# Layer 2 experts: a third buffer of gathered rows, and gathers and index products one group further ahead

## The chip, the cores and the metric

The kernel runs on one core of one Trainium2 chip, in one launch. The core has TensorE (PE) for matmuls, VectorE (DVE), ScalarE (ACT) and GpSimd (POOL) for elementwise work, and SyncE (SP); SP and POOL also issue transfers between the device memory and the on-chip memory. The metric is the time of one execution on the device in microseconds (us); the lower the better.

## The reference

The reference is a network of four layers on 1024 tokens of width 256 (float32). Each layer is a half-weighted feed-forward block, an attention-like block, and the same feed-forward block again. What matters here is the feed-forward block of layer 2, which is computed twice with the same weights ("stage a" and "stage b" below). It is a mixture of 64 experts with 6 choices for each token and room for 64 tokens in each expert:

```python
scores = jax.nn.softmax(xf @ gate_w.T, axis=-1)
topk_w, topk_idx = jax.lax.top_k(scores, K)              # K = 6
# the first CAP = 64 tokens that chose an expert get a place in buf_tok, buf_w
gx = xp[buf_tok]                                          # gather: 64 x 64 rows of 256
gu = jnp.einsum('ech,ehi->eci', gx, gate_up_proj)
g, u = jnp.split(gu, 2, axis=-1)
hid = jax.nn.silu(g) * u                                  # 96 wide
eo = jnp.einsum('eci,eih->ech', hid, down_proj) * buf_w[..., None]
routed = jnp.zeros((T + 1, h), x.dtype).at[buf_tok.reshape(-1)].add(eo.reshape(-1, h))[:T]
shared = jax.nn.silu(xf @ shared_gate_w.T) * (xf @ shared_up_w.T) @ shared_down_w.T
```

## The kernel before

The kernel is a sequence of stages with a barrier of all engines between them. Inside a stage each engine has its own list of instructions, in the order in which the code of that engine writes them, and engines wait for each other only through semaphores. No scheduler moves anything.

The stage in question is `l2_experts_stage`, run once as `l2_ffn_a` and once as `l2_ffn_b`. The trace leaves digits out of names, so its tiles are called `l_ffn_a_...` and `l_ffn_b_...` (so are those of other layers; the line numbers tell them apart). The 64 experts are worked on in 8 groups of 8 experts. A group has 512 places for tokens, in 4 pairs of experts with 128 places each.

What each group g needs, by engine:

- DVE, `one_hot(g, q)` (L3408): for each of the 4 pairs two comparisons, eight 128x512 operations in all (groups 0 and 1: four of 128x1024), into `hot`, which has two buffers.
- PE, `index(g)` (L3234) and `turn_i(g)` (L3241): 32 small matmuls that find for each place its token, then a transpose. For group 0 `index_first` does this pair by pair (L3223).
- DVE, `locate(g)` (L3422 to L3436): turns these sums into row numbers, `take_at` for the gather and `put_at` for the scatter.
- POOL, `take(g)` (L3169): 4 indirect DMAs, each of which gathers 128 rows of 1 KB into `xg`. `take(g)` waits until PE has read the buffer that it writes (`x_filled`), and for `take_at`.
- PE, `turn_x(g)` (L3250): 8 transposes of the gathered rows; ACT, `take_x(g)` (L3362) copies them to `xgT`.
- PE, `up(g)` (L3264): the first product; ACT (L3371) and DVE (L3499) make `hidden`; PE, `turn_h(g)` (L3275), ACT (L3375), PE `down(g)` (L3286): the second product; ACT (L3382) copies it to `eo`, which has two buffers and waits for the scatter of two groups before (`stored`).
- POOL, `put(g)` (L3178): 4 indirect DMAs that scatter 128 rows of 1 KB each into `l2_results`.
- SP loads the weights of a group (1.5 MB and 0.75 MB) three groups ahead, into three buffers.

POOL's list before the change is: take(0), take(1), then for g = 0 to 7 take(g+2) and put(g). PE's is, for each g: up(g), index(g+2), turn_h(g), turn_i(g+2), turn_x(g+1), down(g). DVE's is: hidden(g), locate(g+2), one_hot(g+3), and for g < 6 `weigh(g)` (L3441, L3444). Ahead of the loop PE and DVE have done the index work of groups 0 and 1 and one_hot(2).

After the loop PE computes the shared part (L3212), DVE adds it to `x` (L3486), SP waits until all scatters have landed (L3143) and loads the results back in 8 transfers of 768 KB (L3148), and DVE (L3529, L3546) and PE (L3337) add them to `x`.

## Time and profile before

| | us |
|---|---|
| runs shown | 2226.61, 2211.37, 2215.23 |
| median | 2215.23 |
| profiled execution, its time | 2214.98 |
| profiled execution, its span | 2213.2 |
| mean granted TensorE clock in it | 0.907 |
| stage a, POOL's first gather to its last scatter issued | 867.0 to 976.4 |
| stage b, the same | 1845.6 to 1956.9 |

The profile is of one execution. The span goes from the first to the last instruction and is 1.8 us shorter than the time of the same execution. Over the whole span PE is busy 83% of the time and POOL 21%; these are means over some forty stages with different limits, so the stage itself has to be read.

### The profile page before, as it was taken

The numbers are of one execution on the slowest core, as the hardware profiler recorded it, in microseconds if no ns is written. First come the engines' busy times: TensorE is split into PE (matmuls) and PEld (weight loads), VectorE is DVE, ScalarE is ACT, GpSimd is POOL, SyncE is SP. The second block draws the span as 40 slices with busy tenths as digits, with TensorE's granted clock in tenths as the row PEclk, the third lists the DMA queues.
The fourth block names the chain that finished last, engine by engine and source line by source line (L and its number), as shares of the span: only waits on it lengthen the run. The fifth ranks groups of instructions, "written<-read, shape, count | busy, mean of one in ns | idle before, by whom it ended". The sixth has DMA issues, their size and how long they took to land. (4 is left out here: it accounts for less than half of the span.)

```text
span 2213.2 us, 52159 instructions
## 1 busy us (share of the span) xinstructions
PE 1847.7 (83%) x21053; PEld 1275.8 (58%) x21053; DVE 1218.2 (55%) x3265; ACT 879.8 (40%) x2049; POOL 473.0 (21%) x542
## 2 busy tenths in 40 slices
PE   4886789895999896666999999999999797679669
PEld 1345644563777563554766666666676674446446
DVE  6867532344664336645566666676666226642741
ACT  4523311222552222224666677667666203220120
POOL 0022300330000332642212221222121003720200
PEclk7897989996999997887999999999999798789779
DMA  7000000514200516751000010001000317830000
GB/s 266 18 1 1 1 1 16 176 39 156 111 1 19 177 37 215 246 217 51 21 33 22 22 42 22 22 22 42 22 22 22 84 27 218 262 148 18 1 3 19
DMA packets 55331, 157.37 MB, mean 71 GB/s; under 512 B 12899, under 2 KB 29881, under 8 KB 50822
## 3 DMA queue, kind: packets, MB, share of 16 engines
q1 hardware_dynamic: 45206, 128.84, 17.5%
q0 software_dynamic: 9888, 25.20, 3.4%
q8 instruction: 170, 2.79, 0.5%
q14 instruction: 67, 0.55, 0.1%
HBM read 115.36 MB, written 40.48 MB: 70 GB/s over the span
## 5 line engine op out<-in xcount | busy, mean ns | idle before, releaser
L2362 PE MATMUL l_heads_ps_p<-xnT,l2a_w 128*128 128x512 f32 x512 | 266.3, 636 | 20.5 <-ACT l_heads_shaped L2681 8.1
L2768 DVE SCALAR_TENSOR_TENSOR l_heads_taps<-l_heads_padded,l2a_conv,l_heads_taps 128x1024 f32<-128x1024 f32 x144 | 187.9, 1323 | 9.7 <-ACT l_heads_taps L2595 8.9
L2362 PEld LDWEIGHTS l_heads_ps_p<-xnT,l2a_w 128*128 128x128 f32 x512 | 87.4, 194 | 84.3 <-issue 57.9
L198 PE MATMUL norm_turn<-zeros,ident 128*128 128x512 f32 x120 | 65.1, 698 | 52.1 <-PEq L60 52.1
L2941 POOL TENSOR_TENSOR l_heads_e<-l2a_table,l_heads_row 128x512 f32<-128x512 f32 x32 | 33.3, 1042 | 327.1 <-DVE l_heads_first L2779 325.3
L189 ACT ACT_TABLE_LOAD x10 | 12.8, 1283 | 204.1 <-PEq L60 204.1
L2594 ACT COPY l_heads_padded<-l_heads_ps_p 128x512 f32<-128x512 f32 x96 | 57.1, 595 | 53.6 <-PE l_heads_ps_p L2362 53.6
L2595 ACT ACTIVATE l_heads_taps<-l_heads_ps_p,l2a_conv 128x512 f32<-128x512 f32 x96 | 76.7, 799 | 0.0
L198 PEld LDWEIGHTS norm_turn<-zeros,ident 128*128 128x128 f32 x120 | 25.9, 224 | 85.5 <-issue 85.5
L1984 ACT ACTIVATE l_heads_e<-l_heads_logit,l_heads_shift 128x128 f32<-128x128 f32 (+1 forms) x128 | 56.6, 443 | 44.7 <-DVE l_heads_shift L2016 44.6
L2944 POOL TENSOR_SCALAR_AFFINE_SELECT l_heads_e<-l_heads_e 128x512 f32<-128x512 f32 x64 | 67.0, 1047 | 9.8 <-POOL l_heads_e L2941 0.6
L2779 DVE SCALAR_TENSOR_TENSOR l_heads_first<-l_heads_bank,l2a_table,l_heads_e 128x128 f32<-128x128 f32 x128 | 36.1, 344 | 52.6 <-issue 46.1
L431 PE MATMUL l_ffn_a_ps_gate<-xnT,l_w 128*115 128x512 f32 x44 | 27.5, 760 | 40.5 <-DVE l_w L562 38.7
L2941 POOL TENSOR_TENSOR l_heads_e<-l_heads_row,l2a_table 128x512 f32<-128x512 f32 x32 | 35.3, 1104 | 116.6 <-DVE l_heads_qk L2821 116.6
L2396 PE MATMUL l_heads_bank<-l_heads_mt,l_heads_mz 32*32 32x32 f32 x3072 | 49.2, 193 | 10.9 <-issue 10.9
L2669 ACT ACTIVATE l_heads_k_end<-l_heads_bank,l2a_table 128x128 f32<-128x128 f32 x128 | 36.7, 376 | 35.6 <-PE l_heads_bank L2502 35.6
L1098 DVE TENSOR_TENSOR l_heads_fourth<-l_heads_squares 128x768 f32<-128x768 f32 x32 | 31.0, 968 | 34.8 <-POOL l_heads_squares L994 33.3
L2016 DVE CUSTOM_DVE_ANT_0 l_heads_logit<-l_heads_ps_s,l_heads_mask 128x256 f32<-128x256 f32 (+1 forms) x128 | 40.3, 353 | 16.3 <-PE l_heads_ps_s L1916 16.2
L2396 PEld LDWEIGHTS l_heads_bank<-l_heads_mt,l_heads_mz 32*32 32x32 f32 x3072 | 41.0, 106 | 12.4 <-issue 12.1
L2839 DVE TENSOR_SCALAR l_heads_on<-l_heads_o,l_heads_mean_var,l_heads_rstd 128x128 f32<-128x128 f32 x128 | 35.6, 343 | 22.7 <-POOL l_heads_rstd L2954 22.2
L1058 ACT ACTIVATE l_heads_squares<-l_heads_ps_s 128x768 f32<-128x768 f32 x32 | 25.9, 811 | 54.7 <-PE l_heads_ps_s L1010 54.7
L2025 DVE COPY l_heads_eT<-l_heads_ps_t 128x384 f32<-128x384 f32 x64 | 32.7, 553 | 25.7 <-PE l_heads_ps_t L1925 24.4
(717 smaller groups left out, 4833.8 us busy)
## 6 DMA issues: line engine op xcount, KB each, us to landing
l_results<-zeros SPq DMA_DIRECT2D x24, 512.0 KB, 5.7
l_ffn_a_w_in<-in_l_in_w SPq DMA_DIRECT2D x8, 1536.0 KB
l_ffn_b_w_in<-in_l_in_w SPq DMA_DIRECT2D x8, 1536.0 KB, 10.5
l2a_w<-in_l_w_heads SPq DMA_DIRECT2D x16, 512.0 KB, 3.9
l_heads_row<-l_rows SPq DMA_DIRECT2D x16, 512.0 KB, 4.6
l_ffn_a_w_out<-in_l_out_w SPq DMA_DIRECT2D x8, 768.0 KB
l_ffn_a_w_in<-l_results SPq DMA_DIRECT2D x8, 768.0 KB, 6.5
l_ffn_b_w_out<-in_l_out_w SPq DMA_DIRECT2D x8, 768.0 KB, 8.3
```

The lines of the kernel that those rows point to most:

```text
L198: pe.matmul(turn[:, i % KC, (i // KC) % HALVES, :], core.ident[:], core.zeros[:, 0:HALF], start=True, stop=True)
L1984: act.activation(e[m % 4][:, lo:hi], logit[m % 4][:, lo:hi], ACT.Exp, bias=shift[:, m % 4, j:j + 1], scale=-1.0, accum_out=total[:, n % 4, ...
L2016: dve.tensor_tensor_reduce(logit[m % 4][:, lo:hi], score_bank(n, j)[:, i * width:(i + 1) * width], mask[:, 2 * P - width:], -1.0, LARGEST, ...
L2362: mm = pe.matmul(ps_p[half][:], w[b][:, which, c, :], core.xnT[:, c, half * HALF:(half + 1) * HALF], start=(c == 0), stop=(c == KC - 1))
L2396: mm = pe.matmul(bank[c][1][q, s, 0:BK], m_first(c, s)[q, q] if n == 1 else mz[c][q, s, 0, :], mt[c][q, s, :], start=True, stop=True)
L2594: act.copy(padded[which][:, 2 * half:2 * half + 2, PAD:], src)
L2595: act.activation(taps[which][:, 2 * half:2 * half + 2, :], src, ACT.Identity, bias=conv[b][:, which, TAPS:TAPS + 1], scale=conv[b][:, whic ...
L2669: last = act.activation(dst[:, s, :], tile_of_bank[name][:, s, :], ACT.Copy, scale=columns(h, column, c)[:, s:s + 1])
L2768: dve.scalar_tensor_tensor(out=taps[which][:], in0=padded[which][:, :, j:j + SEQ], scalar=conv[p % 2][:, which, j:j + 1], in1=taps[which][ ...
L2779: last = dve.scalar_tensor_tensor(out=m_first(c, s), in0=tile_of_bank[name][:, s, :], scalar=columns(p, NEG_B, c)[:, s:s + 1], in1=e1[c][: ...
L2941: pool.tensor_tensor(m[:], a, b, ALU.subtract).then_inc(gap_ready, 1)
L2944: pool.affine_select(out=m[:], in_=m[:], compare_op=(ALU.is_gt, ALU.is_ge)[which], fill=DONE_BEFORE, base=0, pattern=[[0, SY], [-sign, P]] ...
```

## The change

`xg` gets a third buffer (`XB = 3`). `take(g)` now waits until group g-3, no longer g-2, has been turned. POOL issues take(0), take(1), take(2) ahead of the loop, and in the loop take(g+3) in front of put(g). For this the row numbers must be there one group sooner: PE computes index(2) and turn_i(2) ahead of turn_x(0) and index(g+3), turn_i(g+3) in the loop; DVE does locate(2) and one_hot(3) ahead of the loop and locate(g+3), one_hot(g+4) in it. The number of instructions of every kind stays the same.

```diff
@@ -3046,7 +3046,8 @@
-        xg = [st.sb(f"xg{b}", [P, PAIRS, D]) for b in range(2)]
+        XB = 3
+        xg = [st.sb(f"xg{b}", [P, PAIRS, D]) for b in range(XB)]
@@ -3096,7 +3097,7 @@
-        x_loaded = [st.sem(f"x_loaded{b}") for b in range(2)]
+        x_loaded = [st.sem(f"x_loaded{b}") for b in range(XB)]
@@ -3161,9 +3162,9 @@
             def take(g, pairs=range(PAIRS)):
-                b = g % 2
-                if g >= 2:
-                    pool.wait_ge(x_filled, g - 1)
+                b = g % XB
+                if g >= XB:
+                    pool.wait_ge(x_filled, g - XB + 1)
@@ -3182,10 +3183,11 @@
             take(0)
             take(1)
+            take(2)
             pool.wait_ge(*cleared)
             for g in range(GROUPS):
-                if g + 2 < GROUPS:
-                    take(g + 2)
+                if g + 3 < GROUPS:
+                    take(g + 3)
                 put(g)
@@ -3241,10 +3243,10 @@
             def turn_x(g):
-                b = g % 2
+                b = g % XB
                 if g >= 1:
                     pe.wait_ge(x_read, KC * g)
-                pe.wait_ge(x_loaded[b], 16 * PAIRS * (g // 2 + 1))
+                pe.wait_ge(x_loaded[b], 16 * PAIRS * (g // XB + 1))
@@ -3317,14 +3319,16 @@
             index(1)
             turn_i(1)
             pe.wait_ge(shared_taken, 2 * UNITS)
+            index(2)
+            turn_i(2)
             turn_x(0)
             for g in range(GROUPS):
                 up(g)
-                if g + 2 < GROUPS:
-                    index(g + 2)
+                if g + 3 < GROUPS:
+                    index(g + 3)
                 turn_h(g)
-                if g + 2 < GROUPS:
-                    turn_i(g + 2)
+                if g + 3 < GROUPS:
+                    turn_i(g + 3)
                 if g + 1 < GROUPS:
                     turn_x(g + 1)
                 down(g)
@@ -3491,6 +3495,9 @@
             locate(1)
             for q in range(PAIRS):
                 one_hot(2, q)
+            locate(2)
+            for q in range(PAIRS):
+                one_hot(3, q)
             for g in range(GROUPS):
...
-                if g + 2 < GROUPS:
-                    locate(g + 2)
                 if g + 3 < GROUPS:
+                    locate(g + 3)
+                if g + 4 < GROUPS:
                     for q in range(PAIRS):
-                        one_hot(g + 3, q)
+                        one_hot(g + 4, q)
```

POOL's list in stage a, from the first gather on (`xg` is written by gathers, `l_results` by scatters). Before:

```order
L3169 DMA l_ffn_a_xg_9547<-l_xn_rows,l_ffn_a_take_at 128x256 x12
L3178 DMA l_results<-l_ffn_a_eo_9547,l_ffn_a_put_at 6144x256 x4
L3169 DMA l_ffn_a_xg_9547<-l_xn_rows,l_ffn_a_take_at 128x256 x4
L3178 DMA l_results<-l_ffn_a_eo_9547,l_ffn_a_put_at 6144x256 x4
L3169 DMA l_ffn_a_xg_9547<-l_xn_rows,l_ffn_a_take_at 128x256 x4
```

And now, to the end of the list:

```order
L3170 DMA l_ffn_a_xg_9547<-l_xn_rows,l_ffn_a_take_at 128x256 x16
L3179 DMA l_results<-l_ffn_a_eo_9547,l_ffn_a_put_at 6144x256 x4
L3170 DMA l_ffn_a_xg_9547<-l_xn_rows,l_ffn_a_take_at 128x256 x4
L3179 DMA l_results<-l_ffn_a_eo_9547,l_ffn_a_put_at 6144x256 x4
L3170 DMA l_ffn_a_xg_9547<-l_xn_rows,l_ffn_a_take_at 128x256 x4
L3179 DMA l_results<-l_ffn_a_eo_9547,l_ffn_a_put_at 6144x256 x4
L3170 DMA l_ffn_a_xg_9547<-l_xn_rows,l_ffn_a_take_at 128x256 x4
L3179 DMA l_results<-l_ffn_a_eo_9547,l_ffn_a_put_at 6144x256 x4
L3170 DMA l_ffn_a_xg_9547<-l_xn_rows,l_ffn_a_take_at 128x256 x4
L3179 DMA l_results<-l_ffn_a_eo_9547,l_ffn_a_put_at 6144x256 x16
```

Sixteen gathers (groups 0 to 3) stand in front of the first scatter where twelve stood, and sixteen scatters (groups 4 to 7) stand behind the last gather where twelve stood.

PE's list in stage a, ahead of the loop and into its first round. Before:

```order
L3234 MATMUL l_ffn_a_bank_l<-l_ffn_a_hot_9547,l_ffn_a_parts 6x128 x32
L3241 MATMUL l_ffn_a_bank_l<-ident,l_ffn_a_by_slot 128x128
L3250 MATMUL l_ffn_a_bank_x_9547<-ident,l_ffn_a_xg_9547 128x128 x8
L3264 MATMUL l_ffn_a_bank_u_9547<-l_ffn_a_w_in_9547,l_ffn_a_xgT_9547 64x192 x16
L3234 MATMUL l_ffn_a_bank_l<-l_ffn_a_hot_9547,l_ffn_a_parts 6x128 x32
```

And now:

```order
L3236 MATMUL l_ffn_a_bank_l<-l_ffn_a_hot_9547,l_ffn_a_parts 6x128 x32
L3243 MATMUL l_ffn_a_bank_l<-ident,l_ffn_a_by_slot 128x128
L3236 MATMUL l_ffn_a_bank_l<-l_ffn_a_hot_9547,l_ffn_a_parts 6x128 x32
L3243 MATMUL l_ffn_a_bank_l<-ident,l_ffn_a_by_slot 128x128
L3252 MATMUL l_ffn_a_bank_x_9547<-ident,l_ffn_a_xg_9547 128x128 x8
L3266 MATMUL l_ffn_a_bank_u_9547<-l_ffn_a_w_in_9547,l_ffn_a_xgT_9547 64x192 x16
L3236 MATMUL l_ffn_a_bank_l<-l_ffn_a_hot_9547,l_ffn_a_parts 6x128 x32
```

The index products and the transpose of group 2 have moved in front of the transposes of the gathered rows of group 0; what follows up(0) are the index products of group 3.

## Rows read from the trace of the kernel before

**Rows 1.** Stretches of stage a: us, busy us (count) of PE, PEld, DVE, ACT, POOL; PEclk, DMA share, GB/s.
```profile
894.00:966.00 72.00, 50.02 (x561) 36.66 (x559) 42.05 (x102) 22.92 (x47) 53.75 (x49) 0.81 0.75 247
...
883.00:894.00 11.00, 8.83 (x91) 7.05 (x93) 2.08 (x10) 2.72 (x6) 0.19 (x1) 0.68 0.21 63
...
918.00:930.00 12.00, 3.99 (x71) 3.00 (x67) 11.36 (x26) 1.83 (x4) 9.62 (x8) 0.76 1.01 345
```

**Rows 2.** Waits of PE in stage a: engine, line, releaser: us in total, times, longest.
```profile
PE l_ffn_a_bank_x L3250 <- DMA l_ffn_a_xg<-l_xn_rows,l_ffn_a_take_at: 22.5, 4, 7.2
```

**Rows 3.** Timeline of POOL, stage a: start, us, instruction, idle before it and releaser.
```profile
894.17 0.95 POOL L3169 DMA_INDIRECT l_ffn_a_xg<-l_xn_rows,l_ffn_a_take_at  x1 [10.98 <-PE l_ffn_a_bank_x L3250]
...
904.79 1.52 POOL L3169 DMA_INDIRECT l_ffn_a_xg<-l_xn_rows,l_ffn_a_take_at  x1 [0.30 <-issue]
...
911.77 1.02 POOL L3178 DMA_INDIRECT l_results<-l_ffn_a_eo,l_ffn_a_put_at  x1 [1.16 <-ACT l_ffn_a_eo L3382]
...
936.16 1.01 POOL L3178 DMA_INDIRECT l_results<-l_ffn_a_eo,l_ffn_a_put_at  x1 [1.29 <-ACT l_ffn_a_eo L3382]
...
965.10 0.98 POOL L3178 DMA_INDIRECT l_results<-l_ffn_a_eo,l_ffn_a_put_at  x1 [1.93 <-ACT l_ffn_a_eo L3382]
...
971.56 0.98 POOL L3178 DMA_INDIRECT l_results<-l_ffn_a_eo,l_ffn_a_put_at  x1 [1.09 <-ACT l_ffn_a_eo L3382]
...
975.43 0.98 POOL L3178 DMA_INDIRECT l_results<-l_ffn_a_eo,l_ffn_a_put_at  x1 [0.30 <-issue]
```

**Rows 4.** Timeline of POOL, stage b.
```profile
1872.96 0.94 POOL L3169 DMA_INDIRECT l_ffn_b_xg<-l_xn_rows,l_ffn_b_take_at  x1 [11.15 <-PE l_ffn_b_bank_x L3250]
...
1890.91 1.02 POOL L3178 DMA_INDIRECT l_results<-l_ffn_b_eo,l_ffn_b_put_at  x1 [1.75 <-ACT l_ffn_b_eo L3382]
...
1915.79 1.02 POOL L3178 DMA_INDIRECT l_results<-l_ffn_b_eo,l_ffn_b_put_at  x1 [2.31 <-ACT l_ffn_b_eo L3382]
...
1938.56 1.02 POOL L3178 DMA_INDIRECT l_results<-l_ffn_b_eo,l_ffn_b_put_at  x1 [0.99 <-ACT l_ffn_b_eo L3382]
...
1945.64 0.98 POOL L3178 DMA_INDIRECT l_results<-l_ffn_b_eo,l_ffn_b_put_at  x1 [2.18 <-ACT l_ffn_b_eo L3382]
...
1952.10 0.98 POOL L3178 DMA_INDIRECT l_results<-l_ffn_b_eo,l_ffn_b_put_at  x1 [1.09 <-ACT l_ffn_b_eo L3382]
...
1955.96 0.98 POOL L3178 DMA_INDIRECT l_results<-l_ffn_b_eo,l_ffn_b_put_at  x1 [0.30 <-issue]
```

**Rows 5.** Timeline of SP and DVE behind the last scatter, stage a.
```profile
977.94 11.90 SPq L3148 DMA_DIRECT2D l_ffn_a_w_in<-l_results  x8
978.05 0.69 DVE L3486 SCALAR_TENSOR_TENSOR x<-l_ffn_a_bank_e,x 128x512 f32<-128x512 f32 x1 [1.03 <-PE l_ffn_a_bank_e L3212]
...
984.19 4.84 DVE L3529 SCALAR_TENSOR_TENSOR x<-l_ffn_a_w_in,l_ffn_a_weight,x 128x256 f32<-128x256 f32 x12 [5.44 <-DMA l_ffn_a_w_in<-l_results]
```

**Rows 6.** Timeline of DVE: comparisons of groups 1 to 4 of stage a, of group 2 of stage b.
```profile
872.06 3.48 DVE L3408 TENSOR_TENSOR l_ffn_a_hot<-l_ffn_a_slot,l_ffn_a_slot_of 128x1024 bf16<-128x1024 bf16 x3
...
877.91 5.05 DVE L3408 TENSOR_TENSOR l_ffn_a_hot<-l_ffn_a_slot,l_ffn_a_slot_of 128x512 bf16<-128x512 bf16 x8
...
893.57 5.10 DVE L3408 TENSOR_TENSOR l_ffn_a_hot<-l_ffn_a_slot,l_ffn_a_slot_of 128x512 bf16<-128x512 bf16 x8
...
902.95 4.90 DVE L3408 TENSOR_TENSOR l_ffn_a_hot<-l_ffn_a_slot,l_ffn_a_slot_of 128x512 bf16<-128x512 bf16 x8
...
1856.56 5.03 DVE L3408 TENSOR_TENSOR l_ffn_b_hot<-l_ffn_b_slot,l_ffn_b_slot_of 128x512 bf16<-128x512 bf16 x8
```

**Rows 7.** Timeline of PE: transposes of index sums, and of group 0's rows in both stages.
```profile
876.71 0.33 PE L3241 MATMUL l_ffn_a_bank_l<-ident,l_ffn_a_by_slot 128*128 128x128 f32 x1 [0.40 <-DVE l_ffn_a_by_slot L3422]
...
883.92 1.94 PE L3250 MATMUL l_ffn_a_bank_x<-ident,l_ffn_a_xg 128*128 128x128 f32 x8 [6.88 <-DMA l_ffn_a_xg<-l_xn_rows,l_ffn_a_take_at]
...
1861.91 1.94 PE L3250 MATMUL l_ffn_b_bank_x<-ident,l_ffn_b_xg 128*128 128x128 f32 x8 [6.23 <-DMA l_ffn_b_xg<-l_xn_rows,l_ffn_b_take_at]
```

**Rows 8.** DMA issues of the stages: KB each, median us from issue to landing.
```profile
l_ffn_a_xg<-l_xn_rows,l_ffn_a_take_at POOLq DMA_INDIRECT x32, 8.1
l_results<-l_ffn_a_eo,l_ffn_a_put_at POOLq DMA_INDIRECT x32, 4.3
```

## The prediction, made before the changed kernel ran

> **What bounds the kernel now.** The changed lines run in the two expert stages of layer 2 only, so I read those and nothing else; everything outside should keep its time. I looked first at the stretches of stage a [rows 1]. In the 72 us from 894 to 966, POOL is busy 53.75 us with 49 indirect DMAs, and each is followed by 0.30 us in which it fetches the next (the idle "issue" of [rows 3]). 53.75 + 49 x 0.30 = 68.5 us of 72: POOL's list is 95% full. PE is busy 50.0 us and DVE 42.1 us in the same stretch, and the DMA engines are at a share of 0.75. The reader should see that POOL, with 21% over the whole span, is the limit of this stage.
>
> The waits of PE [rows 2] seem to say something else: the transposes of the gathered rows wait for the gathers, 22.5 us in 4 waits. But a gather is late there because its turn in POOL's list is late, behind the scatters; so I read POOL's own timeline [rows 3, 4]. Its list begins with gathers 0 and 1 and then stands still for 10.98 us (11.15 us in stage b), until row numbers of group 2 exist. From 894.17 to 975.43 + 0.98 = 976.41 it issues 56 DMAs. In these 82.24 us there are only four waits beyond 0.30 us, all for `eo`, the input of a scatter: 0.86 + 0.99 + 1.63 + 0.79 = 4.27 us. Stage b has five: 1.45 + 2.01 + 0.69 + 1.88 + 0.79 = 6.82 us of the 83.98 from 1872.96 to 1956.94. The rest, 77.97 and 77.16 us, is 56 slots of 1.39 and 1.38 us.
>
> Behind the last scatter the stage has a tail of fixed length [rows 5]: SP starts to load the results back 1.5 us after POOL is done, DVE gets the first at 984.19. So the end of the stage moves with POOL's last scatter, as long as nothing else becomes later than the loads.
>
> **The change, part by part.**
>
> *take(2) leaves the chain: -5.0 us in each stage.* The third buffer lets gather 2 follow gather 1, in the hole in which POOL does nothing. It needs row numbers from locate(2), which needs index(2), which needs one_hot(2). That ends at 877.91 + 5.05 = 882.96 [rows 6]. For group 1 the transpose of the index sums began 1.17 us after the comparisons ended (872.06 + 3.48 = 875.54, then 876.71 [rows 6, 7]), and the row numbers follow it by about 1 us. Gather 2 can be issued from about 885.2 on. Even with four long slots of 1.82 us, as at 904.79 [rows 3] with its 0.30, it is done at 892.5, before the chain starts again. The hole is also empty of transfers: the DMA share is 0.21 from 883 to 894 [rows 1]. What leaves the chain is what take(2) holds in it today: four slots of 0.95 + 0.30 us, 5.0 us.
>
> *The waits for `eo` go: -4.27 and -6.82 us.* Scatter g waits for down(g), which stands in PE's list behind turn_x(g+1), and this waits for gather g+1. Today gather g+1 is issued just before scatter g-1 and gather g+2, so it has two blocks of POOL's list (10 to 11 us) to land, to be turned and to let down(g) and the copy through. Its median from issue to landing is 8.1 us [rows 8], which leaves too little. With the change two more blocks lie between, over 20 us. What is late next is POOL itself.
>
> *Extra work ahead of turn_x(0): +0.45 and +1.1 us.* 32 index matmuls and a transpose now stand in front of it, and they wait for the comparisons of group 2. By the same 1.17 us, and 0.3 for the transpose, turn_x(0) can begin at 884.4 where it began at 883.92, released by its gather; in stage b at 1856.56 + 5.03 + 1.5 = 1863.0 instead of 1861.91 [rows 6, 7]. I take these delays in full for up(0), hidden(0) and the row numbers of group 3, with which gather 3 now opens the chain where gather 2 did.
>
> *The comparisons of group 3 ahead of hidden(0): nothing.* They take 5.1 us [rows 6] from about 885.4, done at 890.5; the input of hidden(0) comes at about that time. If they were late by 1 us, the chain would start 1 us later; the range holds that. In exchange DVE has one round less of them inside the loop.
>
> *More DMAs at once: nothing, with a bound.* No transfer is added. From 894 to 966 the share of 0.75 makes 54 us of transfers [rows 1]. One gather block leaves, some 2 us; the rest has to fit in about 63 us of a shorter chain, a share of 0.83. At its worst (918 to 930) the share is already 1.01 and POOL's slots go on all the same, 9.62 us busy in 12 us. The nearest rows thus bound it between nothing and the return of the waits for `eo`, 11.1 us in both stages. I take nothing, since the new distance hides a landing of twice the median.
>
> *Order on POOL.* Scatter g now stands behind gather g+3 instead of g+2. Counted from the start of the chain, scatters 0 to 4 have as many slots ahead of them as before, scatters 5 to 7 four fewer; the gain of take(2) shows only there. After gather 7 there are 16 scatters in a row instead of 12. Copy eo(g) waits until scatter g-2 has landed: the median is 4.3 us [rows 8], and one scatter block is 5.2 us, so the wait is just covered even there.
>
> *How long a slot is.* This is the one place where rows disagree. Gather 3 at 904.79, beside the comparisons of 902.95 to 907.85, takes 1.52 us; gather 2 at 894.17, beside those of 893.57 to 898.67, takes 0.95 us [rows 3, 6]. Read as it stands, whatever opens the chain is not stretched, so gather 3 would have short slots too, and about three stretches of 0.53 us would go in each stage: 1.6 us twice, a sum of -22.7 us. I don't put this into the sum, because four of the later comparisons remain beside the chain as before and may simply stretch their three slots each; it goes into the range.
> The Trainium skill, page SBUF — State Buffer, section Who interferes with whom, says that a VectorE instruction with two on-chip inputs contends with a GpSimd instruction that reads this memory, and that the second to issue is blocked. By that rule gather 3 beside comparisons of group 4 is stretched, and the sum stays at -19.5 us; the trace agrees at 904.79 and does not at 894.17.
>
> **The sum.** Stage a: -5.0 - 4.27 + 0.45 = -8.8 us. Stage b: -5.0 - 6.82 + 1.1 = -10.7 us. Together -19.5 us. From the profiled execution's 2214.98 us this makes 2195.5 us. The median of the runs shown is 0.25 us above that execution, so it serves for both.
>
> The tail does not take this back: eo(7) needs scatter 5 landed, which is two blocks before POOL's end, so PE's shared part (its last addition on DVE is at 978.05 + 0.69 today [rows 5]) ends some 9 us earlier as well, while the first load comes 7.8 us behind POOL's end.
>
> **The rivals.**
>
> *A. The DMA engines become the limit.* For it: a share of 1.01 at 345 GB/s in one stretch of 12 us [rows 1]. Against: 0.75 over the loop. If landings grow with every gather moved forward, the waits for `eo` come back and only take(2) is won: -10.0 + 1.55 = -8.5 us, 2206.5 us. The Trainium skill, page DMA: Bandwidth & Descriptors, section Issuing engines are not separate DMA queues, says that transfers of all issuing engines run on the same 16 DMA engines and interleave; by it gathers, scatters and weight loads share this limit, and the trace, with one share for all, agrees.
>
> *B. Slower: ACT is caught behind a scatter.* eo(g) waits on ACT until scatter g-2 has landed, and in ACT's list gate(g+1) stands behind it; hidden(g+1), locate(g+4) and gather g+4 hang on that. Today gathers hold PE back so much that no such wait shows. If up to twelve gathers in flight delay scatters, this loop closes. Between the end of scatter g-2 and the start of scatter g lie 12 slots of 1.39 us, 16.7 us; less some 1.7 us for the copy and what follows it, so from a landing of about 15 us on it costs what exceeds 15 us, in 5 rounds of each stage. At 17 us it has eaten the gain (10 x 2 = 20 us against 19.5); at 20 us it is +50 - 19.5 = +30.5 us, 2245.5 us. Against it: a median landing of 4.3 us.
>
> *C. It doesn't do what it says.* Something that I don't see keeps gather 2 out of the hole (row numbers later than 894). Then only delays are left: +1.55 us at most, 2216.5 us.
>
> *D. More than forecast,* by the short slots above: 2192.3 us, or 2190 us if the first wake of POOL is quicker too.
>
> **How the numbers follow.** A measurement of this kernel can tell about 1% (22.2 us) from no change. The forecast, -14 to -22 us, gets 0.58; D 0.19; A 0.12; B 0.05; C 0.06. D is mostly beyond 1% and of the forecast about a tenth: faster by over 1% 0.23. B beyond 1% (a landing from 19 us on) 0.03. Within 1% 0.74. The range reaches from just below D's end, 2188 us, over the forecast to just above A, 2209 us; C, B and a little of each end are left out.
>
> **What would show it right or wrong.** In the changed profile: gather 2 issued between 885 and 893 in stage a, and POOL's idle ahead of gather 3 down from 11 us to 2 or 3; PE's waits for `xg` inside the loop gone, all but group 0's; from gather 3 to the last scatter 52 slots without a wait beyond 0.30 us, 72 us long; last scatter issued near 967.6 in stage a. turn_x(0) beginning 0.4 us later than its gather's landing. A: waits for `xg` that remain. B: idle time of POOL ahead of gathers, released by `take_at`, with ACT waiting for `l_results`. Wrong altogether if slots get longer as transfers get denser: at 1.6 us each instead of 1.39 the 52 slots take back 11 us in each stage, and nothing would be left of the gain.

## The result, and the profile after

| | runs | median, us | lowest to highest |
|---|---|---|---|
| before | 4 | 2217.57 | 2211.37 to 2226.61 |
| changed | 4 | 2193.87 | 2192.65 to 2198.47 |

The ratio is 0.9895, 95% interval 0.9864 to 0.9926: some 23 us less, somewhere between 16 and 30. The profiled execution of the changed kernel took 2192.65 us, its span is 2190.9 us, 22.3 us shorter than that of before.

Not all of these 22.3 us come from the two changed stages. Taken from the first instruction of one stage to that of the next, the span was: ahead of stage a +7.57 us, stage a -7.19 us (160.56 to 153.37), the attention of layer 2 between them -9.05 us, stage b -13.02 us (160.84 to 147.82), the rest -0.61 us. Code that was not touched moved by 8 or 9 us either way from one execution to the next; here the two nearly cancel (-2.1 us). The changed stages gave -20.2 us.

The stretches of stage a (us, busy us and count of PE, PEld, DVE, ACT, POOL; granted clock as a share of 2.4 GHz, DMA share, GB/s). POOL's first gather came 7.8 us later here than in the profile of before (874.82 against 867.01), so the first two windows are those of [rows 1] moved by 7.8 us; three others follow:

```profile
901.80:973.80 72.00, 58.47 (x613) 44.04 (x605) 42.88 (x104) 30.71 (x70) 54.48 (x51) 0.93 0.76 256
890.80:901.80 11.00, 9.22 (x106) 7.15 (x106) 6.67 (x17) 1.74 (x4) 4.48 (x5) 0.52 0.23 69
890.00:896.00 6.00, 3.42 (x43) 2.80 (x45) 4.11 (x13) 1.07 (x2) 2.86 (x3) 0.50 0.21 61
896.00:904.00 8.00, 8.00 (x83) 6.15 (x83) 5.00 (x15) 1.74 (x5) 2.37 (x3) 0.66 0.43 125
930.00:942.00 12.00, 5.50 (x84) 4.09 (x81) 8.89 (x21) 2.79 (x7) 9.56 (x9) 0.88 1.02 345
```

The place of the former hole, 890.8 to 901.8, now holds the four gathers of group 2. The DMA engines are still at only 0.23 in it (0.21 before): these four gathers land within 2.7 to 3.2 us, and much of the stretch stays empty. In the 72 us behind it POOL is as full as before (54.5 us busy, 53.8 before), and PE does 58.5 us of work instead of 50.0, since the same work stands in a shorter stage. The peak of the DMA engines stays where it was, 1.02 at 345 GB/s.

PE's waits in stage a, which answer to [rows 2]:

```profile
PE l_ffn_a_bank_l L3236 <- DVE l_ffn_a_hot L3412: 9.5, 5, 6.1
...
PE l_ffn_a_bank_x L3252 <- DMA l_ffn_a_xg<-l_xn_rows,l_ffn_a_take_at: 4.4, 1, 4.4
```

Waits for gathered rows fell from 22.5 us in four to 4.4 us in one; that one is inside the loop (turn_x(5) at 941.88). In stage b two such waits remain, 5.1 us in all; before there were four there too, 23.7 us. The longest wait is now that of index(2) for its comparisons.

POOL's own list in stage a, for [rows 3]:

```profile
893.79 1.42 POOL L3170 DMA_INDIRECT l_ffn_a_xg<-l_xn_rows,l_ffn_a_take_at  x1 [2.78 <-DVE l_ffn_a_take_at L3435]
...
904.08 0.95 POOL L3170 DMA_INDIRECT l_ffn_a_xg<-l_xn_rows,l_ffn_a_take_at  x1 [5.11 <-PE l_ffn_a_bank_x L3252]
...
914.71 1.52 POOL L3170 DMA_INDIRECT l_ffn_a_xg<-l_xn_rows,l_ffn_a_take_at  x1 [0.30 <-issue]
...
974.58 0.98 POOL L3179 DMA_INDIRECT l_results<-l_ffn_a_eo,l_ffn_a_put_at  x1 [0.30 <-issue]
```

and in stage b, for [rows 4]:

```profile
1855.92 1.41 POOL L3170 DMA_INDIRECT l_ffn_b_xg<-l_xn_rows,l_ffn_b_take_at  x1 [2.79 <-DVE l_ffn_b_take_at L3435]
...
1864.85 0.94 POOL L3170 DMA_INDIRECT l_ffn_b_xg<-l_xn_rows,l_ffn_b_take_at  x1 [3.78 <-PE l_ffn_b_bank_x L3252]
...
1934.97 0.98 POOL L3179 DMA_INDIRECT l_results<-l_ffn_b_eo,l_ffn_b_put_at  x1 [0.30 <-issue]
```

Gather 2 (893.79, 1855.92) runs in what was the hole. Gather 3 (904.08, 1864.85) opens the chain. Between it and the last scatter stand 52 slots, and not one has an idle beyond 0.31 us: 71.48 us in stage a (975.56 - 904.08) and 71.10 us in stage b. From the first gather to the end of the last scatter the list takes 100.74 and 98.99 us (874.82 to 975.56 and 1836.96 to 1935.95) where it took 109.40 and 111.30. This length is the measure used for all experiments below; I call it the list's length.

Behind the last scatter, for [rows 5] (SP, then DVE):

```profile
977.08 12.16 SPq L3149 DMA_DIRECT2D l_ffn_a_w_in<-l_results  x8
```

```profile
983.59 4.84 DVE L3536 SCALAR_TENSOR_TENSOR x<-l_ffn_a_w_in,l_ffn_a_weight,x 128x256 f32<-128x256 f32 x12 [8.80 <-DMA l_ffn_a_w_in<-l_results]
```

The first load is issued 1.5 us behind POOL's end and DVE has its rows 8.0 us behind it (7.8 before): the tail moved along with POOL, as a piece of fixed length.

PE around the opening of the loop, for [rows 7]:

```profile
890.92 1.02 PE L3236 MATMUL l_ffn_a_bank_l<-l_ffn_a_hot,l_ffn_a_parts 128*6 128x128 bf16 x32 [6.07 <-DVE l_ffn_a_hot L3412]
892.34 0.47 PE L3243 MATMUL l_ffn_a_bank_l<-ident,l_ffn_a_by_slot 128*128 128x128 f32 x1 [0.40 <-DVE l_ffn_a_by_slot L3426]
892.61 1.91 PE L3252 MATMUL l_ffn_a_bank_x<-ident,l_ffn_a_xg 128*128 128x128 f32 x8
895.78 5.39 PE L3266 MATMUL l_ffn_a_bank_u<-l_ffn_a_w_in,l_ffn_a_xgT 128*64 128x192 f32 x32 [1.25 <-ACT l_ffn_a_xgT L3366]
901.09 0.77 PE L3236 MATMUL l_ffn_a_bank_l<-l_ffn_a_hot,l_ffn_a_parts 128*6 128x128 bf16 x32
```

turn_x(0) no longer waits for its gather (landed long before) but for index(2). Behind a wait of 6.07 us, index(2), its transpose and turn_x(0) run at a granted clock of 0.50, the lower of the two levels, and so does most of up(0): 0.50 from 890 to 896, 0.66 in the mean from 896 to 904.

The landings, in stage b (median us from issue to landing):

```profile
l_ffn_b_xg<-l_xn_rows,l_ffn_b_take_at POOLq DMA_INDIRECT x32, 7.0
l_results<-l_ffn_b_eo,l_ffn_b_put_at POOLq DMA_INDIRECT x32, 3.0
```

In stage a the median of the gathers is 6.6 us (8.1 in [rows 8]); in stage b of before it was only 3.4 us:

```profile
l_ffn_b_xg<-l_xn_rows,l_ffn_b_take_at POOLq DMA_INDIRECT x32, 3.4
```

Such medians can't be compared. The traces hold a landing for only 16 of the 32 gathers in each stage of before, and for 20 and 12 of them after, of other groups each time. Single gathers landed in 2.7 to 11.3 us in both kernels.

### The profile page after: what moved, and what is told of

Its sections match the earlier page's. It is cut to its first block and busy times, and to the rows that moved or that the text cites. A ratio compares the mean times of both kernels' runs of the same rounds, so it can differ in the third digit from the quotient of the medians.

```text
span 2190.9 us, 52155 instructions
## 1 busy us (share of the span) xinstructions
PE 1844.2 (84%) x21053; PEld 1271.3 (58%) x21053; DVE 1219.1 (56%) x3265; ACT 879.6 (40%) x2049; POOL 472.2 (22%) x542
## 5 line engine op out<-in xcount | busy, mean ns | idle before, releaser
L2362 PE MATMUL l_heads_ps_p<-xnT,l2a_w 128*128 128x512 f32 x512 | 261.2, 625 | 18.5 <-ACT l_heads_shaped L2681 5.9
L1916 PE MATMUL l_heads_ps_s<-l1a_latT,l_heads_qT 128*128 128x512 f32 (+1 forms) x128 | 47.0, 492 | 0.0
```

What stands on the lines that cost most here:

```text
L1916: pe.matmul(score_bank(n, j)[:, 0:2 * width], qT[p % 2][:, b * SEQ + j * P:b * SEQ + (j + 1) * P], latT[:, :, b * SEQ:b * SEQ + width], st ...
L2362: mm = pe.matmul(ps_p[half][:], w[b][:, which, c, :], core.xnT[:, c, half * HALF:(half + 1) * HALF], start=(c == 0), stop=(c == KC - 1))
```

## The experiments

They ran in three groups, each on one chip, with its own runs of the kernel before. Before had its median at 2219.99 us on one, 2214.79 us on another, and 2251.07 us on a third; each was used at one time only, so these runs can't tell the chip from the time. The kernel before was profiled for the first result alone, so the lists' lengths on these three chips have no length of before from the same chip beside them. They come from one profiled execution each; **hole** is POOL's idle in front of the gather that opens the chain.

| kernel | ratio to before [95%] | list a, b, us |
|---|---|---|
| before (profile shown) | | 109.40, 111.30 |
| changed (first result) | 0.9895 [0.9864, 0.9926] | 100.74, 98.99 |
| *chip with 2214.79:* changed again | 0.9897 [0.9867, 0.9927] | 98.05, 101.12 |
| opening gathers late | 0.9929 [0.9903, 0.9955] | 105.18, 104.58 |
| index work alone | 0.9948 [0.9923, 0.9973] | 104.49, 108.45 |
| row numbers of group 3 sooner | 0.9919 [0.9889, 0.995] | 101.67, 102.79 |
| *chip with 2219.99:* third eo | 0.9893 [0.9858, 0.9929] | 100.87, 100.04 |
| half the scatters | 2180.71 us, one run | 88.62, 91.53 |
| fixed rows | 2200.3 us, one run | 97.19, 102.74 |
| fixed rows, no late comparisons | 2193.7 us, one run | 94.81, 99.36 |
| *chip with 2251.07:* changed again | 0.9955 [0.9939, 0.9972] | 122.82, 120.03 |
| third buffer alone | 0.9999 [0.9988, 1.0011] | 126.19, 125.79 |
| index work alone | 0.9996 [0.9983, 1.0009] | 128.88, 129.82 |
| opening gathers late | 0.9997 [0.9985, 1.001] | 129.03, 128.48 |

### The change again, and where each round stalls

On the chip with 2251.07 us. The kernel is the changed one, without any edit.

> The changed kernel once more, on the chip and in the call of the three others, as their measure. In its first trace the two expert stages gave 8.7 and 12.3 us from the first gather to the last scatter (-21.0 us), while unchanged parts of the program moved by +7.8 us ahead of stage a and -7.8 us between the stages. My theory: these two are scatter of one execution, so that the sum over both stages repeats within 1 us, the unchanged parts do not, and the ratio to the kernel before is 0.990. Rival: the two are part of the change (other addresses on chip, other instruction layout) and come again with the same signs and sizes.

2238.76 against 2251.07 us: the gain is there, but half of what it was, and 0.990 lies outside the interval (0.9939 to 0.9972). The list took 22 us longer than in the first result, and its 48 slots from the first scatter on took 88.70 us where they had taken 66.44. In these 48 slots POOL has seven idles of 1.7 to 7.7 us, one in every round but the first. One of them, on DVE, ACT and POOL:

```profile
926.79 0.29 DVE L3426 COPY l_ffn_a_by_slot<-l_ffn_a_bank_l 128x128 f32<-128x128 f32 x1 [3.12 <-DMA l_ffn_b_xs<-l_rows]
```

```profile
926.85 0.58 ACT L3379 COPY l_ffn_a_hiddenT<-l_ffn_a_bank_r 96x512 f32<-96x512 f32 x1 [3.57 <-DMA l_ffn_a_back<-l_results]
```

```profile
928.94 1.00 POOL L3170 DMA_INDIRECT l_ffn_a_xg<-l_xn_rows,l_ffn_a_take_at  x1 [3.29 <-PE l_ffn_a_bank_x L3252]
```

DVE and ACT both copy results of PE, whose matmuls for them began at 922.40 (0.78 us) and 923.72 (0.42 us); both start only at 926.8, within 0.06 us of each other, with releasers that have nothing to do with them. The row numbers, and so POOL's next gather, are late by that. PE's waits show the same (engine, line, releaser: us, times, longest):

```profile
PE l_ffn_a_bank_l L3243 <- DVE l_ffn_a_by_slot L3426: 11.9, 5, 4.2
...
PE l_ffn_a_bank_l L3236 <- issue: 4.1, 7, 1.1
```

"Issue" is PE without work although nothing that the profile shows holds it; neither row of these sizes exists in the first result (by_slot 0.8 us there). So here PE, or what it signals, is late in most rounds (five such waits for `by_slot`, up to 4.2 us), and POOL waits for it. That PE's instructions come late would fit the rows named "issue", but is only argued. The cause stays open: the DMA share over 905 to 975 is only 0.68 there, against 0.75 in the first result, so plain lack of bandwidth is not it.

The Trainium skill, page DMA: Bandwidth & Descriptors, section Issuing engines are not separate DMA queues, says that all issuers share the same 16 DMA engines; that would make transfers late. The rows show engines late, with their data there, so that rule doesn't account for it.

### The third buffer alone

On the same chip.

```diff
-        xg = [st.sb(f"xg{b}", [P, PAIRS, D]) for b in range(2)]
+        XB = 3
+        xg = [st.sb(f"xg{b}", [P, PAIRS, D]) for b in range(XB)]
...
-                if g >= 2:
-                    pool.wait_ge(x_filled, g - 1)
+                if g >= XB:
+                    pool.wait_ge(x_filled, g - XB + 1)
...
```

> The kernel before with the third buffer of gathered rows alone: gather g+2 may overwrite a free buffer, index work and the order of POOL's list stay. My theory: no change (ratio 1.000), since gather 2 waits for its row numbers and not for a buffer, and gathers of the loop wait for their turn; 10.9 us of POOL's idle ahead of gather 2 remain, and so do the four waits for eo of stage a (4.3 us). Rival (the buffer is what held gathers back): the waits for gathered rows, 22.5 us in 4 waits, shrink, and up to 20 us go.

2251.09 us, ratio 0.9999: nothing. On this chip that number alone would say little, since parts of the change that are worth 0.5% and 0.7% elsewhere show nothing here either (below). The profile decides: the hole is as it was before, and gather 2 starts 27.1 us behind the first gather, where it started 27.2 us behind it. Only the releaser has changed:

```profile
894.34 0.95 POOL L3170 DMA_INDIRECT l_ffn_a_xg<-l_xn_rows,l_ffn_a_take_at  x1 [10.91 <-DVE l_ffn_a_take_at L3432]
```

[Rows 3] put the 10.98 us down to PE's transposes, and so to the buffer. But PE had read this buffer by 883.92 + 1.94 = 885.86 [rows 7]; the buffer had been free for 8 us when the gather started. The row numbers had been the last condition all along, as the prediction had it, and freeing the buffer moves nothing.

### The index work alone

Two buffers of gathered rows, POOL's old order; the index products, row numbers and comparisons one group ahead. The edit is shown against the changed kernel. It ran on two chips. First where before takes 2251.07 us:

```diff
-        XB = 3
+        XB = 2
...
             take(1)
-            take(2)
...
-                if g + 3 < GROUPS:
-                    take(g + 3)
+                if g + 2 < GROUPS:
+                    take(g + 2)
                 put(g)
```

> Row numbers one group further ahead, as in the change, but two buffers and POOL's order of before (gather g+2 in front of scatter g). Gather 2 waits only for turn_x(0), which ends about 886.5 in the times of the kernel before, and so goes into the hole. My theory of two terms: the first term is won (gather 2 out of the chain, which now begins with scatter 0 at the first eo), the second is not: gather g+1 still has only two blocks of POOL's list to land, so waits for eo stay or grow, since the chain now starts with a scatter that waits for eo(0). I expect -4 us in stage a and -3 us in stage b, -7 us in all, ratio 0.997. Rival (all of the gain is the filled hole and POOL's list alone decides): -19 us, 0.991.

0.9996 there, in lists of 129 and 130 us with waits of up to 8.2 us in front of scatters; that says nothing on the theory. Then where before takes 2214.79 us:

> Two buffers of gathered rows and POOL's old order; only the index products, row numbers and comparisons stand one group further ahead. Theory: gather 2 waits no longer for row numbers but for turn_x(0) to have read buffer 0, at some 893, so the chain of 56 slots starts 1 us sooner; the waits for eo (4.3 and 6.8 us) stay: -2 us to the kernel before, 0.999. Rival (the row numbers alone open the hole): gather 2 at 888, -12 us, 0.9945.

2205.53 us, 0.9948 [0.9923, 0.9973], and the lists are 4.9 and 2.9 us shorter than those of before. The theory's -2 us is out: it let gather 2 wait for buffer 0 until 893, though turn_x(0) had read it at 886 in the trace of before. The rival's ratio, 0.9945, was met; its -12 us was not, by the lists, since the scatter is late next:

```profile
896.26 1.13 POOL L3170 DMA_INDIRECT l_ffn_a_xg<-l_xn_rows,l_ffn_a_take_at  x1 [4.27 <-PE l_ffn_a_bank_x L3251]
...
904.56 1.47 POOL L3179 DMA_INDIRECT l_results<-l_ffn_a_eo,l_ffn_a_put_at  x1 [3.40 <-ACT l_ffn_a_eo L3385]
```

Gather 2 starts 20.4 us behind the first gather (875.82) instead of 27.2, and then POOL waits 3.1 us beyond the usual 0.30 for the first scatter's input. The later waits for eo stay (3.3 us in stage a, 6.3 us in stage b, against 4.27 and 6.82). So the index work alone gives something over a third of the gain (7.8 of 21 us of the lists). The rest needs the later scatters, and with them the third buffer; whether the index work and the third buffer without the new order would give more was not run.

### The opening gathers late

The change, but gather 2 is held until the row numbers of group 3 exist. The distance between gather and scatter stays; the hole comes back.

```diff
             take(1)
+            pool.wait_ge(take_ready, count_of(3))
             take(2)
```

Where before takes 2251.07 us:

> The changed kernel, but gather 2 is kept back until the row numbers of group 3 are there, so that it stands in the chain again, in front of gather 3. Three buffers, order and index work stay. My theory: only the waits for eo are won (4.3 and 6.8 us) less the delay ahead of turn_x(0): the chain of 56 slots from about the start of gather 3 in the changed kernel, 5.0 us more than the changed kernel in each stage, +10 us against it, -10 us against the kernel before, ratio 0.9955. Rival (the distance alone is the gain, the hole hidden anyway): as fast as the changed kernel, 0.990.

0.9997, with stalls in each round again. Where before takes 2214.79 us:

> The change, but gather 2 waits for the row numbers of group 3, as late as it was before: only the distance in the order is left. Theory: four slots of 1.25 to 1.8 us are back on the chain in each stage, which are 5 us a stage and 10 us in all against the change, ratio to the kernel before 0.9955; the waits for eo stay gone. Rival (the distance gives all): the same time as the change, 0.991. Rival (distance gives nothing): 1.000.

```profile
903.85 1.41 POOL L3170 DMA_INDIRECT l_ffn_a_xg<-l_xn_rows,l_ffn_a_take_at  x1 [12.58 <-PE l_ffn_a_bank_x L3253]
```

2199.95 us. The lists are 105.18 + 104.58 = 209.8 us, against 199.2 for the change on the same chip and 220.7 before: 10.6 us lost to the hole, 10.9 us kept. Both are sums of single executions. Of the 10.6 us, 1.3 us lie ahead of the chain, in when it opens; the chain of 56 slots takes 9.3 us more than that of 52, which in the change's own execution still held 2.6 us of waits for eo. By the whole time 7.6 us are lost against the change. The theory's ratio, 0.9955, lies on the edge of the interval (0.9903 to 0.9955); the rival that nothing is lost, 0.991, lies in it, and only the other one, 1.000, is out. It is the lists that speak against the first rival. The waits for eo are gone in this kernel too, in both stages, so the two parts of the change are separate, and of about the same size.

### A third buffer for eo

The change, with a third `eo` in the storage of `xn`, so that ACT's copy waits for scatter g-3.

```diff
-        eo = [st.sb(f"eo{b}", [P, PAIRS, D]) for b in range(2)]
+        eo = [*(st.sb(f"eo{b}", [P, PAIRS, D]) for b in range(2)), xn[:, 0:PAIRS, :]]
+        EB = len(eo)
```

> The changed kernel with a third buffer eo of expert outputs (the storage of the normalised rows, free once they are stored), so that copy eo(g) waits for scatter g-3 instead of g-2. In the changed kernel ACT waits 9.2 us in 5 waits of stage a for scatters to land. My theory: POOL's list is the limit and never waits, so these waits cost nothing: ratio to the kernel before as for the changed one, 0.990, POOL's 52 slots from gather 3 on still 71.5 us; the waits of ACT go. Rival (ACT caught behind a scatter, which I had as the slower rival): they hold back up(g+1) and what follows, and 5 us or more go.

This asks whether ACT's wait for scatters to land, which grew in the changed kernel, costs anything:

```profile
ACT l_ffn_a_eo L3386 <- DMA l_results<-l_ffn_a_eo,l_ffn_a_put_at: 9.2, 5, 4.1
```

With the third buffer the row is gone, and the lists stay at 100.87 and 100.04 us (ratio 0.9893). 9.2 us of waiting on ACT were worth nothing in them: rival B's loop never closed. In stage b the list still held 1.5 us of waits for eo, so these don't come from ACT's wait for scatters.

### Half of the scatters

The change with pairs 1 and 3 alone scattered; 16 of 32 scatters of each stage are left out, and the counts that SP and ACT wait for are halved.

```diff
-                for q in range(PAIRS):
+                for q in (1, 3):
```

> The changed kernel with the scatters of pairs 0 and 2 of each group left out (16 of 32 in each stage; half of the routed results are missing from the output). If POOL's list is the limit, 16 slots of 1.29 us, 20.6 us, go from it in each stage, and then the next limit shows: DVE's round of 8.4 us for the first five groups and PE's of 6.6 us after them. I expect the last scatter 13 us earlier counted from gather 3, -26 us in both stages against the changed kernel, and PE waiting for hidden and hot, not for DMAs. Rival (the DMA engines or the weights are the limit): less than 8 us in each stage, as only 2 MB of 20 go.

The lists fall by 12.1 and 7.5 us against the first result. But 2.4 us of the first number are a quicker opening. From gather 3 on they fall by 9.7 and 7.6 us, 17.3 us in all, where I had put down 26 us and the rival less than 8 us a stage: the miss is mine in both stages, and in stage b the number is the rival's. The whole time, one run, is 13 us below the change's first result. In the loop PE never waited for weights, and 0.9 and 4.1 us for gathers, so the DMA engines are not the limit either, save perhaps for a part of stage b. 16 slots of 1.29 us did leave POOL's list, and 11.7 and 13.9 us of waits opened in it, most of it in front of the last scatters:

```profile
943.70 0.98 POOL L3179 DMA_INDIRECT l_results<-l_ffn_a_eo,l_ffn_a_put_at  x1 [2.04 <-ACT l_ffn_a_eo L3386]
...
950.14 0.98 POOL L3179 DMA_INDIRECT l_results<-l_ffn_a_eo,l_ffn_a_put_at  x1 [4.17 <-ACT l_ffn_a_eo L3386]
...
956.60 0.98 POOL L3179 DMA_INDIRECT l_results<-l_ffn_a_eo,l_ffn_a_put_at  x1 [4.19 <-ACT l_ffn_a_eo L3386]
```

The last groups come every 6.4 to 6.5 us, which is PE's pace for one group (its transposes of gathered rows start at 939.95 and 946.57 there). So POOL is the limit of this stage, and the next one lies close below it.

### Long slots: with and without the late comparisons

Two kernels. Both scatter to rows worked out ahead, so that the comparisons don't matter for where the scatters go. The second leaves the comparisons of groups 4 to 7 out. These are all the comparisons of the loop; those of groups 0 to 3 are done ahead of it.

```diff
-                if g + 4 < GROUPS:
-                    for q in range(PAIRS):
-                        one_hot(g + 4, q)
```

> The measure for the next run: the changed kernel, but scatters go to fixed rows (one for each place, none out of bounds) instead of the rows that belong to the tokens; the output is not that of the reference. All instructions stay but one more iota. I expect POOL's 52 slots within 1 us of the changed kernel's 71.5 us in stage a, with the same long slots of 1.3 to 1.5 us beside the comparisons.

> As the run with fixed rows, but DVE's comparisons for groups 4 to 7 are left out (32 of 512 elements in each stage; groups 4 to 7 gather the rows found by old comparisons). Theory: the comparisons, with two inputs from the on-chip memory, are what stretches POOL's indirect DMAs from 0.97 to about 1.5 us. Then the ten or so long slots of the loop become short and the 52 slots of stage a take 66 to 67 us instead of 71.5. Rival: slots are long because transfers are dense at that time (share 1.0); then they stay long and the 52 slots take 71 us.

From the first scatter on there are 48 slots. With the comparisons 9 of them in stage a and 10 in stage b are longer than 1.15 us, without them 3 and 3; the 48 keep POOL busy 50.77 and 51.72 us with, 48.47 and 48.29 us without. That is 2.3 and 3.4 us for 6 and 7 long slots, 0.4 to 0.5 us each. Comparisons do stretch POOL's slots. The six long slots that are left stand beside other DVE instructions that began before them and have two inputs as well: the sums of `weigh` (five) and the product for the shared part (one).

Which slots are stretched can be read from when each began. I took all 14 traces and both stages, and all slots beside comparisons of 128x512. Of 214 slots that began 0.03 to 0.34 us behind the start of a comparison all were long, 1.44 us in the mean, and the comparison took 0.68 us. Of 256 slots that began within 0.012 us of the start of one, none was long, 0.96 us in the mean, and it was the comparison that took longer, 0.73 us. The sums can be seen in DVE's rows of the changed kernel, for the comparisons beside gather 3 (short slots) and those of the round behind it (slots of 1.37 to 1.52 us):

```profile
903.48 5.11 DVE L3412 TENSOR_TENSOR l_ffn_a_hot<-l_ffn_a_slot,l_ffn_a_slot_of 128x512 bf16<-128x512 bf16 x8
...
912.86 4.90 DVE L3412 TENSOR_TENSOR l_ffn_a_hot<-l_ffn_a_slot,l_ffn_a_slot_of 128x512 bf16<-128x512 bf16 x8
```

Eight comparisons cost DVE 0.2 us more where POOL's slots stay short; POOL loses 0.4 to 0.5 us in each slot that is stretched.

### The change again, and row numbers of group 3 sooner

On the chip with 2214.79 us. First the change itself:

> The changed kernel once more, for the size of its gain. Theory (POOL's list of 52 slots opens 9 us sooner and has no wait): 20 us in the two stages, ratio 0.991, as long as the engines get their instructions in time; both stages 100 to 101 us and 99 us from first gather to last scatter. Rival (each round has its own stalls on POOL, 2 to 7 us, as where this kernel ran at 2238.76 us): stages of 115 us or more, ratio 0.995 to 0.998.

2192.38 us, 0.9897, as in the first result, and the two lists are 199.2 us together (199.7 there). The code ahead of stage a and between the stages, which had moved by +7.8 and -7.8 us, moved by +1.4 and -2.2 us against before here. So these shifts are scatter from execution to execution and no part of the change, as the theory of the first repetition had it. This execution also shows what the clock does to the hole. PE and POOL in stage a, and PE's clock in the stretch:

```profile
889.35 2.82 PE L3266 MATMUL l_ffn_a_bank_u<-l_ffn_a_w_in,l_ffn_a_xgT 128*64 128x192 f32 x32 [1.25 <-ACT l_ffn_a_xgT L3366]
...
892.46 0.62 PE L3236 MATMUL l_ffn_a_bank_l<-l_ffn_a_hot,l_ffn_a_parts 128*6 128x128 bf16 x32 [0.29 <-DVE l_ffn_a_hot L3412]
```

```profile
895.29 0.95 POOL L3170 DMA_INDIRECT l_ffn_a_xg<-l_xn_rows,l_ffn_a_take_at  x1 [2.74 <-PE l_ffn_a_bank_x L3252]
```

```profile
888.00:895.00 7.00, 5.46 (x82) 4.64 (x83) 6.27 (x17) 2.60 (x6) 3.63 (x4) 0.99 0.45 125
```

Here up(0) ran at the upper level and took 2.82 us; in the first result it took 5.39 us, most of it at the lower one. The hole is 2.74 us instead of 5.11. And in stage b of this execution two waits of [rows 4] came back:

```profile
1910.84 1.94 PE L3252 MATMUL l_ffn_b_bank_x<-ident,l_ffn_b_xg 128*128 128x128 f32 x8 [7.14 <-DMA l_ffn_b_xg<-l_xn_rows,l_ffn_b_take_at]
```

```profile
1923.31 0.98 POOL L3179 DMA_INDIRECT l_results<-l_ffn_b_eo,l_ffn_b_put_at  x1 [1.91 <-ACT l_ffn_b_eo L3386]
...
1929.77 0.98 POOL L3179 DMA_INDIRECT l_results<-l_ffn_b_eo,l_ffn_b_put_at  x1 [1.10 <-ACT l_ffn_b_eo L3386]
```

The last gather of group 6 was issued at 1899.78 and landed 10.9 us later. PE had been waiting for it, and its way from there to the first scatter of group 6 took another 12.5 us, more than the distance in POOL's list covers. POOL lost 1.61 + 0.80 us.

Then the attempt at a better version, which takes index(3) into up(0) and locate(3) between the halves of hidden(0). It also puts turn_i(2) behind turn_x(0):

```diff
             index(2)
-            turn_i(2)
             turn_x(0)
+            turn_i(2)
             for g in range(GROUPS):
-                up(g)
-                if g + 3 < GROUPS:
-                    index(g + 3)
+                if g == 0:
+                    up(0, range(0, 2))
+                    index(3)
+                    up(0, range(2, 3))
+                    turn_i(3)
+                    up(0, range(3, 4))
```

> The change, with the row numbers of group 3 made sooner: index(3) and turn_i(3) stand inside up(0), and locate(3) between the two halves of hidden(0). Theory (what is left ahead of gather 3 is POOL's idle of 5.1 and 3.8 us, on the chain): gather 3 starts some 3 us sooner in stage a and 2 us in stage b, and the stages end 5 us sooner together, ratio to the kernel before 0.988 where the change has 0.991. Rival 1 (hidden(0) comes 2 to 3 us later, so that up(0), down(0) and scatter 0 are late instead): the idle moves ahead of scatter 0 and the stages keep their length, 0 us. Rival 2 (other waits, for xg or eo, open as POOL gets closer to its inputs): half of the 5 us.

Nothing was won, which is rival 1's result. Gather 3 started 28.6 and 29.7 us behind the first gather, where the change on the same chip has 26.9 and 28.1; the lists are 101.67 and 102.79 us, the ratio 0.9919. By the ratio alone the two kernels can't be told apart (the change has 0.9867 to 0.9927). POOL waited for the first scatter, 1.5 and 1.4 us beyond the usual 0.30, as rival 1 says. PE stood inside up(0), waiting for the comparisons of group 3, and gate(0)'s second half (ACT) hung on it:

```profile
895.36 0.62 PE L3236 MATMUL l_ffn_a_bank_l<-l_ffn_a_hot,l_ffn_a_parts 128*6 128x128 bf16 x32 [3.51 <-DVE l_ffn_a_hot L3419]
```

```profile
898.71 0.33 ACT L3382 ACTIVATE l_ffn_a_gate<-l_ffn_a_bank_u 128x192 f32<-128x192 f32 x1 [6.49 <-PE l_ffn_a_bank_u L3266]
```

Where up(0) runs at full clock, index(3) already follows the comparisons at once in the change (892.46, a wait of 0.29 us for `hot`): there the opening is bound by DVE's comparisons, of 5.1 us for a group, and no earlier place for index(3) gets ahead of them. But 1.2 us of the loss have another cause. With turn_i(2) behind turn_x(0) the row numbers of group 2 came later, and with them gather 2 (20.19 us behind the first gather, 18.96 in the change) and the comparisons of group 3. A version with turn_i(2) left in its place was not run. Of the kernels that compute the whole network none was clearly faster than the change.

## Why the prediction was right

2195.5 us were predicted and 2193.87 us measured. Term by term, in us, stage a / stage b, from POOL's rows of before and after:

| term | predicted | measured |
|---|---|---|
| take(2) out of the chain, with the slots' length | -5.0 / -5.0 | -6.49 / -6.06 |
| waits for eo gone | -4.27 / -6.82 | -4.27 / -6.82 |
| the chain opens later | +0.45 / +1.1 | +2.10 / +0.57 |
| sum, first gather to last scatter | -8.8 / -10.7 | -8.66 / -12.31 |

**take(2) leaves the chain: right.** 56 slots took 77.97 and 77.16 us [rows 3, 4], 52 take 71.48 and 71.10 us. The difference is more than four slots of 1.25 us because the four removed were not the only thing: the slots that are longer than 1.15 us without their 0.30 fell from 13 to 11 in stage a and from 12 to 10 in stage b; at 0.4 to 0.5 us each that is most of the rest. The run with the opening gathers late put the term back by itself, 10.6 us for both stages.

**The waits for eo: right, and not for every execution.** They were gone in both stages of the first result. In stage b of four other profiles with the same order of POOL's list, on chips without the stalls (the change again at 0.9897, the third eo, both kernels with fixed rows), 1.5 to 3.6 us of them came back. The cause that I named (two more blocks of POOL's list between gather and scatter) is confirmed by what the late-gather kernel kept, 10.9 us. But "over 20 us" has to hold a landing and PE's way to the scatter, 10.9 + 12.5 us in the case above. My argument from the median of 8.1 us was weak: it is that of 16 gathers of stage a, the four opening ones among them, and stage b, with a median of 3.4 us, had waited longer for eo (6.82 against 4.27 us).

**The later opening: the sign right, the size off in both stages.** Counted from the first gather, turn_x(0) came 0.88 and 1.51 us later (I had 0.45 and 1.1): the chain comparisons, index(2), transpose takes 1.8 us and not 1.5, because index(2) follows a wait of 6 us on PE and runs at a granted clock of 0.50, 1.02 us for the 0.62 at full clock. The other part is one that I had not in the sum: up(0) behind it took 5.39 us in stage a (4.23 before) and 4.13 us in stage b (5.04 before), from when the clock rose. 0.88 + 1.16 = 2.04 of the 2.10, and 1.51 - 0.91 = 0.60 of the 0.57. In stage a this second part is chance of the execution. In the 11 profiles with index(2) ahead of an undivided up(0), up(0) took 2.82 us in six, 4.20 us in one and 5.32 to 5.39 us in four, behind the same instructions at the same times. In stage b it took 4.13 to 4.33 us in all 11, and 5.04 and 5.20 us in the two kernels with the old order on PE, so there the shorter up(0) comes with the change. POOL's idle ahead of gather 3, of which I forecast 2 or 3 us, was 2.74 us in four and 4.96 to 5.12 us in three of the seven profiles with the changed opening in stage a, and 3.78 to 3.99 us in stage b of all seven: there the forecast was never met.

**Comparisons of group 3 ahead of hidden(0): nothing, right by a little.** They ran from 893.69 to 898.74, hidden(0) began at 899.00 after an idle of 0.26 us. With up(0) at full clock they are just in the way: index(3) then waited 0.29 us for them.

**More DMAs at once: nothing, nearly right.** From 904 to 964 the DMA share is 0.84, where I had worked out 0.83. Whether landings became longer is open, for want of comparable records; the single late ones are what counts, as the gather of 10.9 us showed.

**Copy eo(g) behind scatter g-2, "just covered": wrong, at no cost.** ACT waited 9.2 us in five waits for scatters to land in stage a, and 5.3 us in three in stage b; the profile of before has no such wait. Again I had taken a median (4.3 us) for all. The third eo shows that it cost nothing.

**The length of a slot: both readings hold, each for its slots.** Gather 3 at 904.08 ran beside the comparisons of group 4 and took 0.95 us, as did the three behind it, as the row at 894.17 [rows 3] had it. That was rival D, and it was right on these four slots, for 1.1 to 1.5 us a stage. But long slots stayed elsewhere (914.71 above), and leaving the comparisons out removed them. The Trainium skill, page SBUF — State Buffer, section Who interferes with whom, has the second of two contending instructions blocked. The trace agrees where a slot began 0.03 us or more behind a comparison: all 214 were stretched, the comparison was not. Where both began within 0.012 us it was the comparison that was held up, by 0.05 us, and the four opening gathers all began so. That would fit the rule if POOL was first there, but most of the records put the comparison's start a few ns ahead, so it is not shown.

**The rivals.** A (the DMA engines as the limit) and B (ACT behind a scatter) had the right symptoms, one late gather and 9.2 us of ACT's waits, and neither a price in the first result. C is out: gather 2 was issued at 893.79 to 898.97, later than the 885 to 893 that I gave, mostly since the whole stage began 7.8 us later; 19.0 us behind the first gather it is where 886 was in the old trace. For the same reason the last scatter was at 974.58 and not at 967.6: such marks should be given from the stage's first gather on, not from the span's start.

**How much of it is luck.** The lists gave 21.0 us where 19.5 were forecast, because two errors go against each other: 2.6 us too little for the slots, 1.1 us too little for the later opening. That the whole time was met within 2 us also rests on the untouched code, whose shifts of 8 and 9 us happened to cancel in the profiled execution.

**What it did not cover.** On the chip where every round stalls, the change gave 12 us and not 22. Nothing in the profile of before shows this, and the prediction has no term for it.

## What to carry to other kernels

Where one engine's list of DMAs is full, look for the place where it stands empty, and ask which chain of conditions holds the next item there: here a buffer alone moved nothing, the row numbers alone gave a third, and the rest came with the buffer and the new order on top. Split the gain of such a change into what leaves the full list and what no longer waits for a neighbour, since the two can be tested one by one; here they were about equal. Give a prediction's marks from the start of the stage, and judge a change of 1% by the lengths of its own stages, since untouched code moves by 8 us between executions.

## What the runs showed of the hardware that I had not expected

- The same program ran at medians of 2214.79, 2219.99 and 2251.07 us on three chips, each used at one time only. On the slowest the rounds of this stage had stalls of 1.7 to 7.7 us on POOL, one of them traced to results of PE that DVE and ACT got late, for which the profile shows no cause. A change worth 1.0% on two chips was worth 0.45% there, and two halves of it, worth 0.5% and 0.7%, nothing (0.9996 and 0.9997).
- Behind a wait of 6 us on PE the granted clock was 0.50 (1.2 of 2.4 GHz) in all 14 profiles, and it rose at different points: up(0), the same 32 matmuls, took 2.82 to 5.39 us in stage a and 4.13 to 5.20 us in stage b where it was not divided.
- An indirect DMA's slot on POOL that began 0.03 to 0.34 us behind the start of a DVE comparison took 1.44 us instead of 0.96 (214 of 214). When both began within 0.012 us, none of 256 slots was stretched and the comparison took 0.73 instead of 0.68 us.
- The releaser of POOL's wait of 10.98 us was named wrongly (PE's transposes, done 8 us earlier): with that condition gone the wait was 10.91 us, released by DVE's row numbers.
